# A graph layer and a mixture of experts on one core: the expert units' first-layer weight loads move from SyncE's DMA queue to ScalarE's

## The reference, cut to what matters

```python
# x: (8192, 128), adj: (8192, 8192), everything float32
z   = layernorm(x)
msg = z @ W + B
w   = where(adj < 1, exp(-(1/adj - 1)**2 / (2 * 0.5**2)), 0)
x   = x + w @ msg                              # graph layer

h   = layernorm(x)
v   = layernorm(h + moe(h)) * gamma + beta     # expert layer, one sequence of 8192 tokens
x   = x + v

# moe(h): 16 experts, each token goes to its two best ones, 128 -> 256 -> 128
topk_vals, topk_idx = top_k(h @ gate_w + gate_b, 2)
share  = softmax(topk_vals)
expert = relu(h @ w1[e] + b1[e]) @ w2[e] + b2[e]
moe    = sum over the two chosen e of share * expert
```

## Time and profile before

| | |
|---|---|
| median of 3 runs | 1749.46 us (1748.61 to 1751.02) |
| the profiled execution | 1750.74 us |
| its span, first to last instruction | 1748.9 us |
| graph layer (no expert unit yet) | 0 to about 1411 us |
| units of batch 0 sent by POOL | 1442.56 to 1556.6 us |
| pairs 40 to 87 stored by SP | 1553.61 to 1702.1 us |
| POOL's gathers, batch 1 / batch 2 | 1650.29 to 1701.1 / 1705.51 to 1735.6 us |

### The profile page before, as it was taken

How to read it: one execution, slowest core, us unless ns; L and a number is a source line. 1 busy time by engine, 2 the same in 40 slices (tenths; PEclk the granted TensorE clock), 3 DMA queues, 4 the chain that set the end, 5 groups by cost and what they waited for, 6 DMA issues and landing times.

```text
span 1748.9 us, 24960 instructions
## 1 busy us (share of the span) xinstructions
PE 1617.6 (92%) x8210; PEld 1067.8 (61%) x8210; DVE 1464.7 (84%) x2149; ACT 1557.1 (89%) x1483; POOL 469.6 (27%) x375
## 2 busy tenths in 40 slices
PE   4999999999999999999999999999999999777760
PEld 3666666666666666566656665656565669777660
DVE  7999999999999999999999998989899943325556
ACT  5899999999999999999999999999999976445562
POOL 0001040313131322222125213131313017740165
PEclk9999999999999999999999999999999999998795
DMA  9558777777777767676967676767796636778883
GB/s 313 155 169 241 229 207 209 206 217 207 210 204 207 212 202 214 205 213 207 232 197 216 202 211 208 212 209 211 205 229 192 193 105 198 195 179 243 245 232 94
DMA packets 254927, 359.91 MB, mean 206 GB/s; under 512 B 21637, under 2 KB 114315, under 8 KB 254672
## 3 DMA queue, kind: packets, MB, share of 16 engines
q1 hardware_dynamic: 246000, 341.25, 67.8%
q0 software_dynamic: 8800, 17.07, 3.1%
HBM read 323.35 MB, written 31.75 MB: 203 GB/s over the span
## 4 chain that ended last, share of the span: by engine, by line
PE 74%; DVE 8%; SPq 7%; issue 4%; DMA 4%; ACT 2%; POOL 1%; DVEq 0%; POOLq 0%; ACTq 0%
PE acc L1205 46%; PE tp L1224 23%; DVE chunk L735 3%; DMA chunk<-rows_in 3%; SPq L408 3%; DVE chunk L741 2%; SPq L392 2%; POOL chunk L558 1%; PE tp L1255 1%; DVE stats L747 1%; PE acc L1283 1%; PE misc L1181 1%; DMA xs<-in_x_dram 1%; DVE msg L810 1%; SPq L416 1%
## 5 line engine op out<-in xcount | busy, mean ns | idle before, releaser
L1205 PE MATMUL acc<-wT,msg 128*128 128x512 f32 x2048 | 975.6, 599 | 0.0
L591 ACT ACTIVATE wT<-tp 128x1024 f32<-128x1024 f32 x512 | 742.6, 1624 | 16.4 <-PE tp L1224 16.4
L585 ACT ACTIVATE chunk<-chunk 128x2048 f32<-128x2048 f32 x256 | 643.2, 2512 | 0.1
L741 DVE SCALAR_TENSOR_TENSOR chunk<-chunk 128x2048 f32<-128x2048 f32 x256 | 584.8, 2284 | 53.4 <-ACT chunk L585 53.0
L1224 PEld LDWEIGHTS tp<-ident,chunk 128*128 128x128 f32 x4096 | 478.3, 141 | 223.8 <-issue 220.9
L735 DVE SCALAR_TENSOR_TENSOR chunk<-chunk 128x2048 f32<-128x2048 f32 x256 | 583.6, 2280 | 2.1 <-DMA chunk<-in_adj_dram 2.1
L1224 PE MATMUL tp<-ident,chunk 128*128 128x128 f32 x4096 | 533.7, 273 | 0.0
L1205 PEld LDWEIGHTS acc<-wT,msg 128*128 128x128 f32 x2048 | 349.1, 190 | 257.3 <-issue 246.0
L580 ACT ACTIVATE chunk<-chunk 128x4096 f32<-128x4096 f32 x118 | 505.2, 4281 | 0.0
L500 POOL TENSOR_TENSOR pool_carrier<-pool_carrier 1x1 f32<-1x1 f32 x16 | 40.6, 2537 | 783.1 <-DVE row_now L927 783.1
L527 POOL DMA_INDIRECT rows_in<-y_wide,row_now x128 | 208.9, 1632 | 40.8 <-issue 40.8
(11 more groups left out here) (127 smaller groups left out, 803.8 us busy)
## 6 DMA issues: line engine op xcount, KB each, us to landing
chunk<-in_adj_dram SPq DMA_DIRECT2D x256, 1024.0 KB, 5.4
chunk<-in_L_ffn_w_dram SPq DMA_DIRECT2D x176, 128.0 KB, 2.7
chunk<-rows_in SPq DMA_DIRECT2D x176, 64.5 KB, 2.8
rows_out<-chunk SPq DMA_DIRECT2D x48, 128.0 KB, 2.9
y_wide<-y_wide SPq DMA_DIRECT2D x16, 256.0 KB
y_kept<-y_wide SPq DMA_DIRECT2D x16, 256.0 KB, 7.1
chunk<-y_kept SPq DMA_DIRECT2D x16, 256.0 KB, 3.6
chunk<-by_token SPq DMA_DIRECT2D x8, 512.0 KB, 4.9
```

The lines of the kernel that those rows point to most:

```text
L585: act.activation(slot(c), slot(c), ACT.Exp, scale=-1.0).then_inc(inverted, 1)
L591: act.activation(wT[:, (g * PPG + m) % WSLOTS, :], tp[(g * PPG + m) % TSLOTS][:, :], ACT.Exp, scale=-2.0).then_inc(weighted, 1)
L741: dve.scalar_tensor_tensor(out=slot(c), in0=slot(c), scalar=2.0, in1=slot(c), op0=ALU.subtract, op1=ALU.mult).then_inc(squared, 1)
L1205: ins = pe.matmul(acc[:, :], msg[:, n, :], wT[:, (g * PPG + m) % WSLOTS, k * ROWS:(k + 1) * ROWS], start=(n == 0), stop=(n == 2 * PPG - 1))
```

## The change

`load_slot` moves from SP's program to ACT's for units 16 to 175. SP keeps the loads of units 0 to 15 ahead of its loop. In each even step i ACT issues the loads of the units i + 16 and i + 17 behind `copy_rows(i/2+3)` and `relu_hidden(i/2+2)` and ahead of its pieces of the gate and the combination. The reads of `e_tab` into registers for these loads move with them (eleven of twelve). ACT waits for the same event as SP did, the first layer of unit u - 19 (for units 16 to 18, which have no such unit, for the first layer of pair 0).

```diff
@@ SP @@
             def load_slot(u):
-                b = batch_of(u)
-                if u == UNIT0[b]:
-                    sp.wait_ge(table_ready, 2 * b + 2)
-                if u == UNIT0[b] or u % AT_ONCE == 0:
-                    upper = min(u // AT_ONCE * AT_ONCE + AT_ONCE, UNIT0[b + 1])
+                if u == 0:
+                    sp.wait_ge(table_ready, 2)
                     _, values = nc.values_load_multi_w_load_instructions(
-                        e_tab[0:1, u:upper], engines=[mybir.EngineType.SP], ...)
-                    first_layers.update(zip(range(u, upper), values))
-                if u >= SLOTS:
-                    sp.wait_ge(hid_full, (u - SLOTS) // 2 + 1)
-                sp.dma_start(slots[u % SLOTS], w1[bass.ds(first_layers[u], 1), :, :]...).then_inc(slot_full[u % SLOTS], 16)
+                        e_tab[0:1, 0:SLOT_AHEAD], engines=[mybir.EngineType.SP], ...)
+                    first_layers.update(zip(range(SLOT_AHEAD), values))
+                sp.dma_start(slots[u], w1[bass.ds(first_layers[u], 1), :, :]...).then_inc(slot_full[u], 16)
@@ SP's loop @@
                 if i + AHEAD < NU:
                     load_rows(i + AHEAD)
-                if i + SLOT_AHEAD < NU:
-                    load_slot(i + SLOT_AHEAD)
@@ ACT @@
+            def load_slot(u):
+                b = batch_of(u)
+                if u == UNIT0[b]:
+                    act.wait_ge(table_ready, 2 * b + 2)
+                if u == UNIT0[b] or u % AT_ONCE == 0:
+                    upper = min(u // AT_ONCE * AT_ONCE + AT_ONCE, UNIT0[b + 1])
+                    _, values = nc.values_load_multi_w_load_instructions(
+                        e_tab[0:1, u:upper], engines=[mybir.EngineType.Activation], ...)
+                    first_layers.update(zip(range(u, upper), values))
+                act.wait_ge(hid_full, (u - SLOTS) // 2 + 1 if u >= SLOTS else 1)
+                act.dma_start(slots[u % SLOTS], w1[bass.ds(first_layers[u], 1), :, :]...).then_inc(slot_full[u % SLOTS], 16)
@@ ACT's loop @@
                 if i % 2 == 0 and i // 2 + HIDDEN_LEAD < NU // 2:
                     relu_hidden(i // 2 + HIDDEN_LEAD)
+                for u in (i + SLOT_AHEAD, i + SLOT_AHEAD + 1):
+                    if i % 2 == 0 and u < NU:
+                        load_slot(u)
```

More of the change, by code:

```diff
@@ L396, in load_slot @@
             def load_slot(u):
-                b = batch_of(u)
-                if u == UNIT0[b]:
-                    sp.wait_ge(table_ready, 2 * b + 2)
-                if u == UNIT0[b] or u % AT_ONCE == 0:
-                    upper = min(u // AT_ONCE * AT_ONCE + AT_ONCE, UNIT0[b + 1])
+                if u == 0:
+                    sp.wait_ge(table_ready, 2)
                     _, values = nc.values_load_multi_w_load_instructions(
-                        e_tab[0:1, u:upper], engines=[mybir.EngineType.SP], min_val=0, max_val=E - 1,
+                        e_tab[0:1, 0:SLOT_AHEAD], engines=[mybir.EngineType.SP], min_val=0, max_val=E - 1,
                         skip_runtime_bounds_check_because="a count of experts, clamped to the last one")
-                    first_layers.update(zip(range(u, upper), values))
-                if u >= SLOTS:
-                    sp.wait_ge(hid_full, (u - SLOTS) // 2 + 1)
-                sp.dma_start(slots[u % SLOTS], w1[bass.ds(first_layers[u], 1), :, :].rearrange("a h f -> (a h) f")).then_inc(slot_full[u % SLOTS], 16)
+                    first_layers.update(zip(range(SLOT_AHEAD), values))
+                sp.dma_start(slots[u], w1[bass.ds(first_layers[u], 1), :, :].rearrange("a h f -> (a h) f")).then_inc(slot_full[u], 16)
             def store_rows(q):
@@ L655, in copy_rows @@
                 act.activation(rT[q % RT], t_bank[q % T_BANKS], ACT.Copy).then_inc(rT_ready, 1)
+            first_layers = {}
+            def load_slot(u):
[5 more added lines that the diff above has]
+                    _, values = nc.values_load_multi_w_load_instructions(
+                        e_tab[0:1, u:upper], engines=[mybir.EngineType.Activation], min_val=0, max_val=E - 1,
+                        skip_runtime_bounds_check_because="a count of experts, clamped to the last one")
+                    first_layers.update(zip(range(u, upper), values))
+                act.wait_ge(hid_full, (u - SLOTS) // 2 + 1 if u >= SLOTS else 1)
+                act.dma_start(slots[u % SLOTS], w1[bass.ds(first_layers[u], 1), :, :].rearrange("a h f -> (a h) f")).then_inc(slot_full[u % SLOTS], 16)
             hidden_biases = {}
```

## The result

| | before | after |
|---|---|---|
| median, us | 1750.10 (1748.61 to 1751.02) | 1721.88 (1718.96 to 1722.98) |
| ratio, 95% interval | | 0.9837, 0.982 to 0.9854 |
| span of the profiled execution, us | 1748.9 | 1721.2 |
| last send of batch 0 starts | 1555.62 | 1555.67 |
| pair 46 stored | 1571.79 | 1562.78 |

The account below looks back on a forecast made before the run. SP's issue time was taken as the bound after 1557 us, the DMA engines not far behind. Gains of 11 + 11 + 2 = 24 us (17.5 to 30) gave 1725.5 us, own range 1719 to 1732, stated range 1714 to 1742.

Parts of the forecast that it names:

- pairs 46 to 67: Stretch between SP's stores of these pairs: from 3.58 to 3.05 us a pair over 21 pairs, 11 us gained (7.5 to 14.3).
- from there to batch 2's gathers: Pairs 68 to 87: POOL becomes the later one at about 54.4 us, against 58.5 today; gain 0 to 4 us, 2 taken.
- tail from there: From batch 2's first gather to the end: 24 gathers at POOL's pace and the last group, 43.4 us, unchanged.
- SP is the bound: After 1557 us SP's issue time bounds; without two 0.52 us weight loads a plain pair falls from 2.54 to 1.50 us.
- The rival of no change: Rows stay late because SP spends what it gains waiting for DVE in `store_rows`: 1749.5 us; chance 0.09.
- ACT's cost: Loads issued on ACT overlap its relus: 0.65 us allowed an issue, some 2.1 us a pair; upper bound 3.1 us.
- the third rival: ACT becomes the bound if it can't issue while activations run; slower above 0.63 us an issue, 1771 at 0.75; chance 0.07.
- its own formula: With ACT as the bound, batch 2's gathers start at 1596.5 + 174 d us, d being one issue on ACT.
- The signal that the prediction named for it: ACT's copies coming over 1 us after PE's transposes in each pair would show that ACT is the bound.
- Catch-up: End of batch 0: SP keeps up with POOL, so pair 46 is stored at about 1560.8 us, 11 us earlier (10 to 12).
- I take 0.95: DMA share assumed for pairs 46 to 67, giving 3.05 us a pair; 0.90 gives 7.5 us gain, 1.0 gives 14.3.
- With SP free the DMA engines are next: Pairs 46 to 67: DMA engines limit next; 234 GB/s at share 0.81 means 2.90 us a pair at share 1.0.

## Why the prediction was right, and where it was off

| step | predicted | measured |
|---|---|---|
| pair 46 earlier | 11 us | 9.0 |
| pairs 46 to 67 | 11 us (7.5 to 14.3) | 17.8 |
| from there to batch 2's gathers | 2 us (0 to 4) | 1.0 |
| tail from there | 43.4 us, unchanged | 43.5 |
| sum | 24 us (17.5 to 30) | 27.7 |

**SP is the bound.** Right: with its issue time put back the gain is zero. SP's plain pair was put at 1.50 us and takes 1.46. The rival of no change falls, yet its wait is there: SP waits for DVE more than twice as long, and PE still waits 29.6 us for rows.

The Trainium skill, "DMA: Bandwidth & Descriptors", section "Issuing engines are not separate DMA queues", calls the sequencer's time for an issue usually small relative to the DMA itself. An issue takes 0.52 us of SP and the weights land after 3.8, so this trace agrees with the sentence; but 160 such issues in one full queue were worth the whole 28 us.

**ACT's cost.** The allowance of 0.65 us an issue and some 2.1 us a pair was on the safe side for plain pairs (0.51 us apart, 1.6 to 1.9 us a pair). The overlap read from the earlier trace rows is there. What was wrong is the distance: the third rival got 0.07, and its outcome begins with the next two issues. By its own formula the first gather of batch 2 at 1720.3 us in that run answers to d = (1720.3 - 1596.5) / 174 = 0.71 us for a load and the issue behind it, past the stated 0.63. The signal that the prediction named for it was bad too. From pair 46 to 67 in PE's and ACT's time lines, 9 of the kernel after's 21 copies start more than 1 us behind their transpose (median 0.84, up to 2.2; in the kernel before 0.04), with the kernel 28 us faster; with the further issues it is 11 of 21 (median 1.2). What tells the cases apart is whether PE waits for the copies, 1.7 us in the kernel after against 19.9:

```profile
PE tp L1266 <- ACT msg L648: 1.7, 3, 0.8
```

The Trainium skill, "Perfetto Trace Analysis", section "DMA Instruction — HWDGE (DVE, Sync)", has an issue wait for the lock of a shared generator. With two sequencers issuing, ACT's median is 340 ns and its least 339: in the typical issue nothing of such a wait shows, and only single ones are long, up to 1881 ns. Those need no second sequencer: SP alone had some, up to 1712 ns.

**Catch-up.** 2 us short, and the mis-sized term is the landing of POOL's last send. DVE's add of unit 91 in its time line:

```profile
1560.86 0.29 DVE L1080 TENSOR_TENSOR chunk<-acc,blobs 128x128 f32<-128x128 f32 x1 [1.99 <-DMA by_token<-chunk]
```

It is 5.2 us after the send at 1555.67, where 3.3 was taken from the landing of a store: 1.9 of the 2.0 us. The prediction says that a scatter's landing has no row, but the trace of the kernel before has some. There the add of unit 78 waits for the scatter of unit 66, 12 units back, and comes 5.3 us behind its send (POOL's and DVE's time lines):

```profile
1538.98 0.97 POOL L534 DMA_INDIRECT by_token<-chunk  x1 [0.30 <-DVE chunk L1069]
...
1544.32 0.29 DVE L1069 TENSOR_TENSOR chunk<-acc,blobs 128x128 f32<-128x128 f32 x1 [2.97 <-DMA by_token<-chunk]
```

The adds from 1523 to 1553 us that wait for a scatter come 3.0 to 5.3 us behind its send, so 3.3 was near the low end.

**Pairs 46 to 67.** The step that failed in its size is "I take 0.95" with the end at a share of 1.0. The share is no ceiling (1.01 here, 1.02 without the combination), and 17.8 us lie outside the bound of 14.3. A share of 1.01 by itself would give 14.9 us; the other 2.9 are bytes per share, 234 / 0.81 = 289 GB/s before and 308 / 1.01 = 305 after, which the scaling by the share held fixed. The rate does better, though it is picked with the result known. 234 GB/s for 75.2 us are 17.6 MB; at the 305 GB/s of the best 10 us in the earlier trace rows they take 57.7 us, and 57.4 were measured. "With SP free the DMA engines are next" is shown only in part: half the weights' bytes gave 0.9 us of the stretch, and what the lists of ACT and DVE do beside them the prediction did not see.

**Landing and POOL.** The last store of batch 1 was issued 5.5 us before the gather that waits for it, instead of 3.3: 2.2 us lost. POOL became the later one as foreseen, and the two gathers' starts lie 52.05 us apart in place of 55.22: 3.2 us won. The sum is 1.0.

So the time came out 3.6 us below the forecast, by 6.8 us from the pace, less the 2.0 of the catch-up and 1.0 behind pair 67 (the small rest is the tail and the step from span to median). The mechanism was right; that the sum stayed inside 17.5 to 30 us is in part luck, as the pace alone left its bounds and the other two steps took 3 us back.

## What to carry to other kernels

Count the issue time of a DMA queue like an engine's work: 0.52 us for each of two loads, in a list of 3.6 us a pair that hardly waited, was the bound, though it stands in no engine's busy time. Before moving issues to another engine, ask how much of its own work they can hide behind; here two a pair nearly fitted behind ACT's relus and four did not, a difference of 43 us. And for "what is next" take bytes over the best rate that the trace shows rather than a share of 1.0, and look for a second limit just behind it before promising what the next change will bring.

## What the runs showed of the hardware that was not expected

At the higher rate the loads land later. The DMA issues from pair 46 to 67 (operation, engine, count, KB each, median us to landing), before and after:

```profile
chunk<-in_L_ffn_w_dram SPq DMA_DIRECT2D x42, 128.0 KB, 3.8
...
chunk<-rows_in SPq DMA_DIRECT2D x42, 64.5 KB, 3.6
```

```profile
chunk<-in_L_ffn_w_dram ACTq DMA_DIRECT2D x44, 128.0 KB, 5.4
...
chunk<-rows_in SPq DMA_DIRECT2D x42, 64.5 KB, 5.5
```

From 233 to 308 GB/s the rows' landing goes from 3.6 to 5.5 us. The rate is not all of it: with SP's small DMAs put back it was 4.4 us at 234 GB/s. A forecast that fills the DMA engines has to lengthen its landings as well, and this one, which kept 3.3 us for the last store of batch 1, was 2.2 us short there. (The scatter of the catch-up took as long before the change.)

POOL, idle in this stretch, issued the same loads at 1.13 us for two, 0.56 each, about as fast as SP (0.52) or ACT (0.51). From its time line in the run with 40 loads on POOL:

```profile
1559.99 1.13 POOL L556 DMA_DIRECT2D chunk<-in_L_ffn_w_dram  x2 [1.19 <-PE tp L1283]
```
